# Half of an up projection moved ahead of the transposes of the probabilities, in the second slot of each batch

## What is computed

```
x  = x + xattn(layernorm(x), ctx, mask)       # scores, masked softmax over 64, readout
n  = layernorm(x)
h  = silu(linear_bit(n, w1, g1)) * linear_bit(n, w2, g2)      # 512 -> 2048
out = x + linear_bit(h, w3, g3)                                # 2048 -> 512
linear_bit(x, w, g): rmsnorm with gain g, rows rounded to 8 bit steps,
                     w rounded to {-1, 0, 1} times one factor, matmul
```

## Time and profile before

| | us |
|---|---|
| median of 3 runs | 444.42 (443.5 to 445.0) |
| profiled execution, its own time | 444.06 |
| its span, first to last instruction | 442.3 |
| PE busy | 398.4 |
| DVE busy | 382.3 |
| POOL busy | 358.3 |
| ACT busy | 343.5 |

### The profile page before, as it was taken

The page is one execution under the profiler, slowest core; times in us unless marked ns, Lnnn a source line. Parts: engine busy times, 40 slices in busy tenths (PEclk is TensorE's granted clock), DMA queues, the critical chain, the costliest instruction groups (busy, mean ns, idle before and its releaser), DMA issues.

```text
span 442.3 us, 8289 instructions
## 1 busy us (share of the span) xinstructions
PE 398.4 (90%) x1870; PEld 179.0 (40%) x1870; DVE 382.3 (86%) x835; ACT 343.5 (78%) x618; POOL 358.3 (81%) x559
## 2 busy tenths in 40 slices
PE   8326596899999999999999999999999989999996
PEld 8102232334434443444344444444344443444443
DVE  5599598999799979997999979997999799798794
ACT  3677779687998789886998698878988697667661
POOL 0149888999889988898879987998889897899970
PEclk9755796999999999999999999999999999999999
DMA  6999881545675547843684568554784425354541
GB/s 256 398 333 367 282 189 24 143 90 125 171 194 103 119 105 188 184 103 81 170 194 92 117 168 189 105 119 102 183 185 103 88 66 113 80 96 101 106 103 73
DMA packets 110359, 66.40 MB, mean 150 GB/s; under 512 B 100736, under 2 KB 100864, under 8 KB 106752
## 3 DMA queue, kind: packets, MB, share of 16 engines
q1 hardware_dynamic: 110336, 66.14, 58.5%
HBM read 33.10 MB, written 8.39 MB: 94 GB/s over the span
## 4 chain that ended last, share of the span: by engine, by line
PE 53%; POOL 13%; DVE 12%; ACT 10%; issue 9%; DVEq 1%; DMA 1%; POOLq 0%; SPq 0%; ACTq 0%
PE S L1279 29%; PE DN L1312 15%; POOL stageB L549 5%; PE R L1258 3%; ACT stageB L740 3%; DVE stageB L972 3%; ACT prob L695 2%; DVE hm L978 2%; POOL c L538 2%; ACT L695 2%; PE DN L1320 1%; DVE ga L945 1%; PE R L1225 1%; ACT junk_x L718 1%; ACT sg L748 1%
## 5 line engine op out<-in xcount | busy, mean ns | idle before, releaser
L549 POOL TENSOR_TENSOR stageB<-stageB,g3b 128x512 f32<-128x512 f32 x127 | 161.9, 1289 | 7.4 <-DVE stageB L972 4.8
L1279 PE MATMUL S<-W2q,q12T 128*128 128x512 f16 x512 | 134.2, 385 | 5.3 <-DVE W2q L1044 3.3
L1279 PE MATMUL S<-W1q,q12T 128*128 128x512 f16 x512 | 135.9, 389 | 1.2 <-ACT sg L748 0.9
L1312 PE MATMUL DN<-W3q,stageB 128*128 128x512 f16 x496 | 122.2, 380 | 0.5 <-DVE W3q L1044 0.4
L748 ACT ACTIVATE sg<-S,asc 128x512 f32<-128x512 f32 x128 | 86.9, 682 | 25.5 <-PE S L1279 23.4
L972 DVE TENSOR_TENSOR stageB<-sg,S 128x512 f32<-128x512 f32 x128 | 86.1, 678 | 20.0 <-ACT sg L748 20.0
L978 DVE TENSOR_REDUCE hm<-stageB 128x1 f32<-128x512 f32 x127 | 85.9, 677 | 2.0 <-POOL stageB L549 1.9
L1279 PEld LDWEIGHTS S<-W2q,q12T 128*128 128x128 f16 x512 | 50.4, 99 | 69.4 <-DVE W2q L1044 4.5
L1279 PEld LDWEIGHTS S<-W1q,q12T 128*128 128x128 f16 x512 | 48.8, 100 | 70.2 <-issue 9.2
L1312 PEld LDWEIGHTS DN<-W3q,stageB 128*128 128x128 f16 x496 | 47.9, 98 | 59.1 <-issue 1.1
L755 ACT ACTIVATE junk<-stageB 128x1024 bf16<-128x1024 f32 x64 | 67.3, 1051 | 4.3 <-DVE stageB L972 4.2
(11 more groups left out here) (127 smaller groups left out, 431.1 us busy)
## 6 DMA issues: line engine op xcount, KB each, us to landing
X<-in_x SPq DMA_DIRECT2D x8, 1024.0 KB, 6.3
out_x<-X SPq DMA_DIRECT2D x32, 256.0 KB, 2.7
xTs<-in_xT SPq DMA_DIRECT2D x7, 1024.0 KB, 7.2
X<-in_w1T SPq DMA_DIRECT2D x4, 1024.0 KB, 10.7
stageB<-in_w2T SPq DMA_DIRECT2D x4, 1024.0 KB, 18.5
X<-in_w3T SPq DMA_DIRECT2D x4, 1024.0 KB, 9.2
ctxr<-in_ctx SPq DMA_DIRECT2D x16, 128.0 KB, 3.0
ctxc<-in_ctx SPq DMA_DIRECT2D x8, 128.0 KB, 4.4
```

The source lines that it names most:

```text
L549: nc.gpsimd.tensor_tensor(gh[q][:, part], hp[:, part], g3b[:, part], ALU.mult).then_inc(s_gh_made, 1)
L1279: mm = nc.tensor.matmul(bank[n % 2][:, :], q12T[q][:, i * KD + k, :], w[:, n, k, :], start=(k == 0), stop=(k == KD - 1))
L1312: mm = nc.tensor.matmul(bank[:, :], src[:, k, :], W3q[:, k, :], start=(k == 0), stop=(k == KH - 1))
```

## The change

`up` gets two more arguments, the first half to do and how many. In the slots with attention and j = 1 the W1 half of chunk 2 stands ahead of attention_probT and the W2 half behind it; before, both stood behind. All else keeps its order, on PE and on the other engines.

```diff
-            def up(t, n, q):
-                if n == 0:
+            def up(t, n, q, first=0, count=2):
+                if n == 0 and first == 0:
                     pe.wait_ge(s_q12_in, 16 * (t + 1))
                 for i, (bank, w, wq, done, used) in enumerate(((S1, W1q, s_w1_q, s_up1_ps, s_silu_made),
                                                                (S2, W2q, s_w2_q, s_up2_ps, s_hp_made))):
+                    if not first <= i < first + count:
+                        continue
...
                 if attn and j == 1:
+                    up(t, 2, q, 0, 1)
                     attention_probT(a)
+                    up(t, 2, q, 1, 1)
                 if attn and j == 2:
                     attention_readout(a, 1)
-                up(t, 2, q)
+                if not (attn and j == 1):
+                    up(t, 2, q)
                 down(t - 2, 2, 2)
```

## The result

The changed kernel is slower: 446.47 us (445.56 to 448.52, 7 runs) against 444.32 us (443.43 to 445.0, 7 runs), a ratio of 1.0056 with a 95% interval of 1.0036 to 1.0076. The forecast was 441.8.

What follows compares the result with a forecast made beforehand. PE, busy 46.9 of 47.9 us per batch, bounds the kernel; 6 x 0.86 = 5.2 us, cut by the DMA landing to 2.5, gives 441.6, or 441.9 against the median, stated as 441.8; range 440.8 to 443.1, 8 in 10: 439.7 to 444.9.

Steps and rivals of the forecast that it cites:

- The hole: PE's gap between the down matmuls and the transposes (line 1246), 1.23 us in batch 2; the 0.86 us W1 half fits.
- the six: The six slots changed (tiles 5, 9, 13, 17, 21, 25): five of batches 1 to 5, one of batch 6.
- The full worth of 5.2 us: Gain if all 0.86 us of the W1 half is saved behind the transposes in each of six slots.
- the landing of the transposed half: DMA of transposed q3 before the next slot's down matmuls, 3.1 to 3.4 us; leaves 2.5 of 5.2 us.
- what reaches the end: Behind that DMA up to the scores: no PE wait as near, POOL lags by at most 0.2 us, so 2.5 stays.
- Rival C: DVE lines 916 and 945 stretch beside POOL as phase changes, 1.0 us in five batches: slower, 446.9 us; chance 0.13.
- the ring: A batch's cycle: PE from probabilities to next scores, then ACT and DVE from copy to exponentials, then PE again.
- Its threshold: Rival C's stretch decides from 0.5 us per batch on, and is measurably slower from 0.76 on.
- A: Full gain: the DMA landing isn't the limit, so all 5.2 us count; 438.9 to 440.5 us, chance 0.10.
- B: PE's new wait for the q3 DMA takes all the gain; 443.2 to 444.9, around 444.4 us; chance 0.21.
- B's second form: POOL, which lets only 0.31 us per batch pass, holds the ring together with a late landing; within B's 0.21.
- D: The W1 half waits for something unseen, so the transposes come late by what was gained; 444.4 us, chance 0.04.

Runs made afterwards that it cites:

- a_hold2: Changed kernel; in each batch's third slot POOL's first gain_3 (line 549) waits until DVE has finished the gain steps (line 945): 442.16 us, ratio 0.9946.
- a_pad: Changed kernel with the W2 half behind the transposes done twice (eight matmuls in place of four, same result): 444.32 us, ratio 1.0001.
- a_hold23_q: a_hold23 plus a swap on ACT in the second slot, first quantize_3 half ahead of the third chunk's silu: 440.92 us, ratio 0.9912.
- a_hold23: Changed kernel; in the third and fourth slots POOL's first gain_3 (line 549) waits until DVE has finished the gain steps: 442.64 us, ratio 0.996.
- a_hold3: Changed kernel; in the fourth slot only POOL's first gain_3 (line 549) waits until DVE has finished the gain steps: 444.21 us, ratio 0.9994.
- b_q: Kernel before the change; on ACT in the second slot, first quantize_3 half ahead of the third chunk's silu: 444.52 us, ratio 1.0002.

## Why the prediction was wrong

**What held.** The hole takes the W1 half: the wait at line 1246 fell from about 1.07 to 0.20 us (a_hold2, a_pad), and in the first of the six it vanished; in the changed kernel itself it is 0.64, as the exponentials come 0.44 later behind the longer subtraction. The full worth of 5.2 us was cut by the landing of the transposed half, in the order of the size forecast: 2.0 us of new wait in six, and a_hold23_q shows that it was this landing. Where nothing else happens the change gives 444.4 - 442.2 = 2.2 us (a_hold2) or 1.8 (a_hold23); forecast were 2.5. A batch of a_hold23 takes 47.5 to 47.7 us instead of 47.98, which is the 0.3 to 0.5 less that was foretold.

**The step that failed** is in the part on what reaches the end: POOL "is moved 0.31 where PE is moved up to 0.5, and falls behind by at most 0.2". The sum had no term for it. I compared POOL with PE, and looked at one idle time of POOL in the fourth slot. What counts is POOL against DVE, and one slot earlier, and there POOL didn't fall behind but came forward. From the subtraction to the third slot's gain steps the view shows no idle time of DVE, in either kernel, and DVE didn't move at all (gain steps 12.72 us behind the transposes in both), while POOL there waits for ACT's square, and that for PE. The row was in the trace of the kernel before and I had not used it:

```profile
177.25 0.20 POOL L554 TENSOR_TENSOR hs<-hss 128x1 f32<-128x1 f32 x1 [0.73 <-ACT junk L755]
```

0.73 us that POOL could come forward; it came 0.49 against DVE. Before, gain_3 started 182.27 - 181.89 = 0.38 us behind the end of the gain steps.

**Rival C** had the mechanism, a DVE step stretched by a change of phase against POOL, and was given 0.13. It had the direction wrong: it let POOL fall behind DVE, and at the gain steps POOL came forward. POOL does fall behind at the subtraction: by 0.44 us in the changed kernel, as a consequence of the meeting, and by 0.28 in a_hold23_q without one. It named line 916, which became 0.44 us longer, and a stretch of 1.0 us, which came, but twice per batch and outside the last stretch of the ring, where DVE's idle time took part of it. Its price of 5.0 us was the price of one stretch per batch fully on the ring; the true loss against the clean case is 446.5 - 442.2 = 4.3 us: 2.05 for the subtraction and 2.3 for the second gain step. That its 446.9 lies so near the measured 446.5 is luck. Its threshold, 0.5 us per batch, was right in size (4.3 / 5 = 0.86 was lost). I had argued against it that part of the stretch was "paid already"; the gain steps of the third and fourth slot had paid nothing.

**Rivals A and B.** A is refuted by the wait for the DMA: the full lead came only when that DMA was issued earlier (a_hold23_q). B (the DMA wait takes all) is refuted by a_hold23, where that wait is as long and the kernel gains. B's second form, POOL holding the ring by its own small room, is not what a_hold2 shows: POOL keeps up there, and the gain comes. D is refuted by the fallen wait.

**The shared interfaces.** The sentence on the SBUF interfaces that POOL shares with VectorE (the Trainium skill, GPSIMD Engine Reference, section 1, Specifications) stood beside C. The runs agree with it: the lines that stretch read two tensors from SBUF, and the stretch goes when POOL is kept off them. The price here was 1.0 us for a gain step.

**A wait, not a slow-down.** Two pairs of rows, the kernel before and then the changed one:

```profile
210.10 2.51 POOL L549 TENSOR_TENSOR stageB<-stageB,g3b 128x512 f32<-128x512 f32 x2
...
212.17 0.72 DVE L916 TENSOR_TENSOR sd<-sm,smax 128x256 f32<-128x256 f32 x1
```

```profile
211.76 2.50 POOL L549 TENSOR_TENSOR stageB<-stageB,g3b 128x512 f32<-128x512 f32 x2
...
213.38 1.16 DVE L916 TENSOR_TENSOR sd<-sm,smax 128x256 f32<-128x256 f32 x1
```

The subtraction ends 0.28 us behind the end of POOL's gain_3 in both (212.89 and 212.61; 214.54 and 214.26), though it overlaps gain_3 for 0.44 us in one and 0.88 in the other. In batch 6 of a_hold3 it overlaps for 1.12 us, takes 1.40, and again ends 0.28 behind. A step that merely ran slower beside POOL would have less left to do after a longer overlap. The gain pairs that begin ahead of gain_3 all end 0.53 to 0.56 us behind it. So the later of the two instructions waits for the earlier one to end.

**What stays open.** How the first meeting brings on the others is known in part. In the changed kernel POOL's gain_3 waits longer for DVE's gate (14.6 us in 22 against 3.6 in six), and in the first slot its end lies 0.88 us behind the start of the subtraction instead of 0.44. Why the fourth slot's gain steps follow those of the third was seen (a_hold2) and not taken apart further.

## What to carry to other kernels

A lead that one engine gains moves the engines that wait for it and leaves those that don't: before costing the gain, list for each engine in the stretch whether it moves, and look where two steps that stretch each other will then stand side by side. When the result has the same instructions and more busy time, compare durations by line first; the group whose time grew names the culprit. And if an edit loses, try to put only the disturbed pair apart by one wait: here that turned a loss of 2.1 us into a gain of 2.2, and with the next wait moved too, into 3.5. Go through the durations again after each gain: in the last kernel the subtraction is longer than before the change.

## What the runs showed of the hardware

- A DVE step of 0.75 us (two inputs in SBUF, 128x512 f32) took 1.76 us when it came behind the start of a POOL tensor_tensor of 1.27 us; the subtraction of 128x256 took 0.43 us alone and 0.72 to 1.40 beside POOL. The other side pays as well: POOL's tensor_tensor of 128x2 took 0.61 us beside the gain steps and 0.19 otherwise.
- Line 972 (one input in SBUF, one in PSUM) and the reduction in line 978 (one input in SBUF) showed no such spread: 0.67 to 0.69 us before and after the change.
- Start-up differs from run to run by 0.7 us before the first changed instruction (transposes of batch 1 at 119.78, 120.34 and 120.49 us in the kernel before, the changed kernel and b_q); a difference of that size between the times of two profiles needn't come from the change.
